# A mixture-of-experts kernel: the find products in fp32r over 128 rows, experts split over the halves of the partitions

## The chip, the cores and the metric

One Trainium2 chip, one of its cores. The metric is the kernel's time on the device in microseconds (us); the median of three runs before the change is 3870.12 us.

## The reference, cut to what matters

One layer on x of shape (4, 2048, 512), so 8192 tokens: a state-space part (layer norm, convolution, projections, a scan over the sequence), and then a mixture of experts with a shared expert. The second part is what the change touches:

```python
idx_flat = topk_idx.reshape(-1)                  # 8 of 64 experts per token
sort = jnp.argsort(idx_flat)
tok = sort // TOPK
x_sorted = x_flat[tok]
group_sizes = jnp.bincount(idx_flat, length=e).astype(jnp.int32)
g = jax.lax.ragged_dot(x_sorted, we_gate, group_sizes)
u = jax.lax.ragged_dot(x_sorted, we_up, group_sizes)
o = jax.lax.ragged_dot(jax.nn.silu(g) * u, we_down, group_sizes)
w_sorted = topk_w.reshape(-1)[sort].astype(o.dtype)
y = jnp.zeros_like(x_flat).at[tok].add(o * w_sorted[:, None])
```

All of it is float32.

## The kernel before, in words

The work goes in stages, one after the other, each a block of its own in which all engines run. `constants` makes index rows and masks. `ssm_inputs` and `scan_states` do the state-space part. `token_tiles` goes through 16 groups of four tiles of 128 tokens: it finishes the layer's first half, does the shared expert, picks the experts, and counts. `tile_table` turns the counts into a table of up to 576 expert tiles. `expert_tiles` goes through these 576 tiles, each 128 places of one expert.

**Counting.** The 8192 tokens are 64 blocks of 128. For every group of `token_tiles`, `count` multiplies the 0/1 matrix of chosen experts by a triangle: for each block, expert and slot, how many tokens of the block up to that slot chose the expert, less the same of the block before. ScalarE copies the sums out of PSUM (`keep_counts`, L939), SyncE stores them in DRAM as `rank_counts` (`store_counts`, L672). At the end `load_ranks` (L676) reads them back with the block as the partition: `k.ranks`, [64 blocks, 64 experts, 130], bfloat16; two more columns per expert hold a count of what lies ahead and a step in token numbers. The loads come in two parts: blocks 0 to 55 before the last two groups' counts are stored, the last eight after. Behind them in SyncE's order are the stores of the last two groups' weights (L668); the last of these waits for GpSimd's `weigh` (L747).

**The table.** `tile_table` begins with three products of `k.ranks`' last count column (L1291 to L1293), on which VectorE's first step (L1213) waits. Later two pairs of products (L1300, L1302) spread each expert's begin over its tiles; VectorE makes `k.begin` [64, 640] (L1284) and `k.rank` [128, 640] (L1286) of them.

**Finding.** For each expert tile the kernel must find which 128 tokens it holds. `mark` (L1727, VectorE, four tiles at once) compares each slot's number with `k.begin` and writes `past`, [64 blocks, 4 tiles, 128 slots] of 0 and 1 in bfloat16. `find` (L1535, TensorE) multiplies it for each tile by `k.ranks` of the tile's expert, 64 rows, 128 columns of weights, 130 moving columns, into `ps_find`. The expert's number is read by TensorE's sequencer out of the table (`expert_of`). `pick` (L1734 to L1743, VectorE) turns the sums into token numbers, for two tiles at once.

**The expert tile.** TensorE's order is written out by hand in `step`: `turn_x` of the next tile (four fp32 transposes, L1523), then in every fourth step `find` for four tiles twelve ahead, `gate_up` of this tile (twelve fp32r products of 512 columns, L1553, in three quarters: high by high, high by low, low by high), `turn_h` of the tile before (two transposes, L1582), `down` of the one before that (six products, L1572). Products in full accuracy are sums of three fp32r ones, with weights and inputs split into a high and a low part by ScalarE (L1632, L1640, L1656) and VectorE (L1695, L1703, L1709). SyncE loads new weights (L1460), GpSimd gathers the tokens' rows (L1489) and adds the results into the output (L1497). VectorE's order in `step` is: the low part of the next x, the low parts of new weights, then at s == 1 and s == 3 `pick`, at s == 2 `mark`, then `hidden` (L1715), `keep_h_low`, `scale` (L1722). Three groups of `mark`, `find` and `pick` stand ahead of the loop as a prologue.

```python
pe.wait_ge(marked, i + SHORT)
after(pe, picked, i)
for t, e in enumerate(experts):
    last = nc.tensor.matmul(ps_find[t // 2][:, t % 2, :], past[:, t, :],
                            k.ranks[:, bass.ds(e, 1), :].rearrange("j o t -> j (o t)"), ...)
```

Of the kernel before, what the change touches and what calls it, by code (L numbers as in the profile page):

```python
# [34 lines left out]
NEG = -3.0e38  # L35

# [19 lines left out]
def constants(nc, k):  # L56

    with ExitStack() as ctx:
        ahead_i = ctx.enter_context(nc.sbuf_tensor("ahead_i", [NB, NB], I32))
        ahead = ctx.enter_context(nc.sbuf_tensor("ahead", [NB, NB], F32))  # L60
        left_i = ctx.enter_context(nc.sbuf_tensor("left_i", [NB, P], I32))
        row_i = ctx.enter_context(nc.sbuf_tensor("row_i", [P, TABLE], I32))
        rank_i = ctx.enter_context(nc.sbuf_tensor("rank_i", [P, TABLE], I32))
        slot_i = ctx.enter_context(nc.sbuf_tensor("slot_i", [NB, P], I32))
        block_i = ctx.enter_context(nc.sbuf_tensor("block_i", [NB, 1], I32))
        block_f = ctx.enter_context(nc.sbuf_tensor("block_f", [NB, 1], F32))
        in_group = ctx.enter_context(nc.sbuf_tensor("in_group", [NB, 1], F32))
        is_first = ctx.enter_context(nc.sbuf_tensor("is_first", [NB, 1], F32))
        step = ctx.enter_context(nc.sbuf_tensor("step", [NB, 1], F32))
# [31 lines left out]
        def _(dve):  # L101
# [4 lines left out]
            nc.vector.tensor_scalar(ahead[:], ahead_i[:], 0.0, None, ALU.max)  # L106
            nc.vector.tensor_copy(k.left[:], left_i[:])
# [19 lines left out]
            nc.vector.tensor_copy(k.ranks[:, :, P + 1], step[:].to_broadcast([NB, E]))  # L127
# [406 lines left out]
def token_tiles(nc, k):  # L534
# [3 lines left out]
    with ExitStack() as ctx:  # L538
# [54 lines left out]
        counts = sb("counts", [E, 2, SUB, P], BF16)  # L593
# [62 lines left out]
        def _(sp):  # L656
# [18 lines left out]
            def load_ranks(at, to):  # L675
                sp.dma_start(k.ranks[at:to, :, 0:P], k.counts[at:to]).then_inc(ranks_loaded, 16)  # L676
# [43 lines left out]
            sp.wait_ge(ranks_loaded, 32)  # L720
# [430 lines left out]
def tile_table(nc, k):  # L1151
# [4 lines left out]
    with ExitStack() as ctx:  # L1156
# [32 lines left out]
        base = sb("base", [E, NB])  # L1189
# [5 lines left out]
        ps_step = ps("ps_step", [NB, E])  # L1195
        ps_turned = ps("ps_turned", [E, 2, P])
        ps_begin = [ps(f"ps_begin{i}", [NB, 512]) for i in range(2)]
# [3 lines left out]
        totalled = ctx.enter_context(nc.semaphore("q_totalled"))  # L1201
        upto_made = ctx.enter_context(nc.semaphore("q_upto_made"))
# [7 lines left out]
        def _(v):  # L1210
# [31 lines left out]
            nc.vector.tensor_scalar(base[:], ps_base[:], begins[:], None, ALU.add).then_inc(begins_made, 1)  # L1242
# [39 lines left out]
            for i, (at, to) in enumerate(((0, 512), (512, TABLE))):  # L1282
                v.wait_ge(spread_out, 2 * i + 2)
                nc.vector.scalar_tensor_tensor(out=k.begin[:, at:to], in0=k.tile_row[0:NB, at:to], scalar=float(-P),  # L1284
# [4 lines left out]
        def _(pe):  # L1289
            totals = k.ranks[:, :, P - 1]  # L1290
            nc.tensor.matmul(ps_total[:], k.left[:], totals, start=True, stop=True).then_inc(totalled, 1)  # L1291
            nc.tensor.matmul(ps_base[:], totals, k.ahead[:], start=True, stop=True).then_inc(totalled, 1)
            nc.tensor.matmul(ps_step[:], k.is_ahead[:], totals, start=True, stop=True).then_inc(totalled, 1)  # L1293
# [5 lines left out]
            for i, (at, to) in enumerate(((0, 512), (512, TABLE))):  # L1299
                nc.tensor.matmul(ps_begin[i][:, 0:to - at], base[:], of_tile[:, at:to], start=True,  # L1300
                                 stop=True).then_inc(spread_out, 1)
                nc.tensor.matmul(ps_first[i][:, 0:to - at], begins_row[:], of_tile[:, at:to], start=True,  # L1302
                                 stop=True).then_inc(spread_out, 1)
# [10 lines left out]
def expert_tiles(nc, k):  # L1314
# [8 lines left out]
    with ExitStack() as ctx:  # L1323
# [25 lines left out]
        past = sb("past", [NB, SHORT, P], BF16)  # L1349
# [165 lines left out]
        def _(pe):  # L1515
# [10 lines left out]
            def expert_of(i):  # L1526
                return pe.snap(entry(pe, i, 0, 2 * WSLOTS * E - 1) // (2 * WSLOTS), min_val=0, max_val=E - 1)
# [161 lines left out]
        def _(v):  # L1689
# [35 lines left out]
            def mark(i):  # L1725

                nc.vector.tensor_tensor(past[:], k.slot_row[:].unsqueeze(1).to_broadcast([NB, SHORT, P]),  # L1727
                                        k.begin[:, bass.ds(i, SHORT)].unsqueeze(2).to_broadcast([NB, SHORT, P]),
# [150 lines left out]
```

## Time and profile before

| | us |
|---|---|
| median of three runs | 3870.12 |
| lowest, highest | 3867.17, 3877.96 |
| the profiled execution | 3868.12 |
| its span in the trace | 3866.4 |
| mean granted TensorE clock | 0.973 |

How to read it: PE is TensorE's matmuls, PEld its weight loads, which overlap the matmuls; DVE is VectorE, ACT ScalarE, POOL GpSimd, SP SyncE; a q behind a name is that engine's sequencer. Matmuls are pipelined: their starts are recorded, their ends are modelled, so the length of one says less than the distance from start to start. In a merged row "x4" four follow each other, and the length is from the first one's start to the last one's modelled end. True fp32 products show as two records of weight load and two of matmul each, fp32r and bfloat16 products and transposes as one.

### The profile page before, as it was taken

How to read it: one execution, taken by the hardware profiler on the slowest of the kernel's cores; microseconds unless marked ns; L12 is line 12 of the kernel's file. 1: busy time of each engine (PE TensorE's matmuls, PEld its weight loads, DVE VectorE, ACT ScalarE, POOL GpSimd, SP SyncE). 2: the span in 40 equal slices, each digit the busy share in tenths (PEclk: the TensorE clock that was granted, in tenths of full speed). 3: DMA queues.
4: the chain of work that ended last, by engine and by line, in shares of the span. 5: the costliest groups of instructions: out<-in, count | busy, mean ns of one | idle time of the engine just before them, and what ended most of it. 6: DMA issues, size and time to landing. Idle time of an engine off the chain costs nothing.

```text
span 3866.4 us, 111487 instructions
## 1 busy us (share of the span) xinstructions
PE 3562.0 (92%) x17240; PEld 2854.9 (74%) x17241; DVE 2334.4 (60%) x5857; ACT 1389.3 (36%) x4103; POOL 1688.9 (44%) x1372
## 2 busy tenths in 40 slices
PE   5929888679999999999999899999999999999996
PEld 3417777558777877887888687888887877787785
DVE  5467777555666665666555655666555566566553
ACT  2234333223334333343333433333333333334331
POOL 1011111135555554555555454555555555555543
PEclk9969999889999999999999999999999999999998
DMA  3323333246667666676666666666666677667654
GB/s 125 102 82 120 113 110 106 77 104 135 135 146 174 142 137 139 123 172 151 123 124 154 159 116 129 142 139 139 126 142 121 142 159 164 136 126 169 122 102 74
DMA packets 216893, 502.58 MB, mean 130 GB/s; under 512 B 46847, under 2 KB 46975, under 8 KB 216456
## 3 DMA queue, kind: packets, MB, share of 16 engines
q0 software_dynamic: 129024, 320.94, 43.8%
q1 hardware_dynamic: 86472, 176.21, 13.6%
q10 hardware_dynamic: 1344, 4.85, 0.4%
q8 instruction: 18, 0.29, 0.0%
q14 instruction: 35, 0.29, 0.0%
HBM read 1115.79 MB, written 191.41 MB: 338 GB/s over the span
## 4 chain that ended last, share of the span: by engine, by line
PE 61%; DVE 5%; issue 5%; ACT 3%; DVEq 2%; DMA 2%; ACTq 2%; POOLq 0%; POOL 0%; SPq 0%
PE e_ps_gu L1553 35%; PE e_ps_y L1572 16%; PE e_ps_x L1523 5%; DVE e_w_low L1695 3%; PE e_ps_h L1582 3%; ACT e_w_high L1632 2%; PE e_ps_find L1535 2%; DMA out<-e_y,e_y_ids 1%; DVEq L1417 1%; ACTq L1417 1%; DVE e_past L1727 1%; DVE e_y L1722 1%; DVE e_below L1738 0%; DVEq L1695 0%; ACT e_xT_high L1640 0%
## 5 line engine op out<-in xcount | busy, mean ns | idle before, releaser
L1497 POOL DMA_INDIRECT out<-e_y,e_y_ids x576 | 956.3, 1660 | 1319.4 <-ACT e_weight L1644 603.7
L1553 PE MATMUL e_ps_gu<-e_w_high,e_xT_high 128*128 x2304 | 688.7, 419 | 15.6 <-issue 6.0
L1489 POOL DMA_INDIRECT e_x<-token_rows,e_x_ids x576 | 610.4, 1060 | 205.9 <-issue 172.8
L1553 PE MATMUL e_ps_gu<-e_w_low,e_xT_high 128*128 x2304 | 648.4, 400 | 6.3 <-issue 4.7
L1553 PE MATMUL e_ps_gu<-e_w_high,e_xT_low 128*128 x2304 | 653.0, 402 | 0.9 <-issue 0.6
L1722 DVE TENSOR_SCALAR e_y<-e_ps_y,e_weight 128x512 f32 (+1 forms) x576 | 431.0, 748 | 254.1 <-PE e_ps_y L1572 249.4
L1703 DVE TENSOR_TENSOR e_xT_low<-e_ps_x,e_xT_high 128x512 fp32r<-128x512 f32 x576 | 397.6, 690 | 266.5 <-ACT e_xT_high L1640 185.9
L1553 PEld LDWEIGHTS e_ps_gu<-e_w_high,e_xT_low 128*128 128x128 f32 x2304 | 430.8, 190 | 129.5 <-issue 29.2
L1553 PEld LDWEIGHTS e_ps_gu<-e_w_low,e_xT_high 128*128 128x128 f32 x2304 | 429.9, 189 | 126.7 <-issue 31.3
L1651 ACT ACTIVATE e_silu<-e_ps_gu 128x256 f32<-128x256 f32 x576 | 221.2, 384 | 827.3 <-PE e_ps_gu L1553 790.8
L1553 PEld LDWEIGHTS e_ps_gu<-e_w_high,e_xT_high 128*128 128x128 f32 x2304 | 396.5, 191 | 98.4 <-issue 37.4
L1640 ACT CAST e_xT_high<-e_ps_x 128x512 fp32r<-128x512 f32 x576 | 336.5, 584 | 302.1 <-PE e_ps_x L1523 301.4
L1572 PE MATMUL e_ps_y<-e_w_high,e_hT_high 128*128 x1152 | 411.6, 438 | 0.0
L1715 DVE TENSOR_TENSOR e_h<-e_silu,e_ps_gu 128x256 f32<-128x256 f32 x576 | 241.7, 420 | 280.6 <-ACT e_silu L1651 268.7
L1523 PEld LDWEIGHTS e_ps_x<-ident,e_x 128*128 128x128 f32 x2304 | 366.7, 204 | 54.9 <-issue 5.2
L1523 PE MATMUL e_ps_x<-ident,e_x 128*128 128x128 f32 x2304 | 366.0, 281 | 5.2 <-DVE e_xT_low L1703 5.0
L1572 PE MATMUL e_ps_y<-e_w_high,e_hT_low 128*128 x1152 | 362.8, 396 | 0.0
L1572 PE MATMUL e_ps_y<-e_w_low,e_hT_high 128*128 x1152 | 362.4, 396 | 0.0
L1660 ACT CAST e_x_ids<-e_tile_ids (+1 forms) x576 | 110.1, 192 | 506.1 <-issue 393.7
L1582 PEld LDWEIGHTS e_ps_h<-ident,e_h 128*128 128x128 f32 x1152 | 226.5, 197 | 53.0 <-DVE e_h L1715 4.5
L1695 DVE TENSOR_TENSOR e_w_low<-e_w_raw,e_w_high x128 | 226.0, 1766 | 50.9 <-issue 26.6
L1572 PEld LDWEIGHTS e_ps_y<-e_w_high,e_hT_low 128*128 128x128 f32 x1152 | 218.1, 189 | 51.1
(284 smaller groups left out, 4123.1 us busy)
## 6 DMA issues: line engine op xcount, KB each, us to landing
e_w_raw<-in_L_ffn_we_gate SPq DMA_DIRECT2D x576, 512.0 KB
e_w_raw<-in_L_ffn_we_up SPq DMA_DIRECT2D x576, 512.0 KB
e_w_raw<-in_L_ffn_we_down SPq DMA_DIRECT2D x576, 512.0 KB
a_x<-in_L_attn_x SPq DMA_DIRECT2D x64, 256.0 KB, 3.4
t_x_in<-in_L_attn_x SPq DMA_DIRECT2D x64, 256.0 KB, 2.7
token_rows<-t_xn SPq DMA_DIRECT2D x64, 256.0 KB, 2.0
out<-t_y_out SPq DMA_DIRECT2D x64, 256.0 KB, 2.1
e_x<-token_rows,e_x_ids POOLq DMA_INDIRECT x576
```

The lines of the kernel that those rows point to most:

```text
L1489: pool.indirect_dma_start(x[:, s % XS, :], None, k.rows, bass.IndirectOffsetOnAxis(x_ids[:, s:s + 1], 0)) \
L1497: pool.indirect_dma_start(k.out, bass.IndirectOffsetOnAxis(y_ids[:, s:s + 1], 0), y[:, s % YS, :], None, compute_op=ALU.add).then_inc(adde ...
L1523: last = nc.tensor.transpose(ps_x[:, c, :], chunks[:, c, :], k.ident[:])
L1553: last = nc.tensor.matmul(ps_gu[s % 2][:], x[:, s % 2, c, :], w[:, c], start=(n == 0), stop=(n == 3 * DC - 1))
L1572: last = nc.tensor.matmul(ps_y[s % 2][:], x[:, s % 2, c, :], w[:, c], start=(n == 0), stop=(n == 3 * FC - 1))
L1582: last = nc.tensor.transpose(ps_h[:, c, :], chunks[:, c, :], k.ident[:])
L1640: nc.scalar.copy(xT_high[:, s % 2], ps_x[:]).then_inc(xT_high_ready, 1)
L1651: nc.scalar.activation(silu[:, s % 2, :], ps_gu[s % 2][:, 0, :], ACT.Silu).then_inc(silu_ready, 1)
L1695: split_weights(v, words, s, lambda half, place: nc.vector.tensor_tensor(w_low[:, bass.ds(place, 1), PARTS[part]], w_raw[:, bass.ds(half, ...
L1703: nc.vector.tensor_tensor(xT_low[:, s % 2], ps_x[:], xT_high[:, s % 2].bitcast(F32), ALU.subtract).then_inc(xT_low_ready, 1)
L1715: nc.vector.tensor_tensor(h[:, s % 2, :], silu[:, s % 2, :], ps_gu[s % 2][:, 1, :], ALU.mult).then_inc(h_made, 1)
L1722: nc.vector.tensor_scalar(y[:, bass.ds(slot, 1), :].rearrange("p o d -> p (o d)"), ps_y[s % 2][:], weight[:, s % SHORT:s % SHORT + 1], Non ...
```

## The change

The counts stay in float32 from PSUM to SBUF, and `k.ranks` becomes fp32r. Its 128 partitions are now the 64 blocks twice: the lower 64 hold experts 0 to 31, the upper 64 experts 32 to 63, [128, 32, 130], so it takes as many bytes per partition as before. `past` becomes [128, 4, 128] in fp32r, and a find product goes over 128 rows; of the half of the rows that belong to the other experts, `k.begin` is 2^20 too large, so that `past` is 0 there (`not_half`, added to `base`). `expert_of` takes the expert's number modulo 32. The first products of the table become fp32 ones, two of 64 rows each, and the constants for them are made for 128 partitions. Each load of the ranks becomes two, one for each half.

```diff
--- before.py
+++ after.py
@@ constants
...
-        left_i = ctx.enter_context(nc.sbuf_tensor("left_i", [NB, P], I32))
+        left_i = ctx.enter_context(nc.sbuf_tensor("left_i", [P, P], I32))
...
-            nc.vector.tensor_scalar(ahead[:], ahead_i[:], 0.0, None, ALU.max)
-            nc.vector.tensor_copy(k.left[:], left_i[:])
+            for rows, first in ((slice(0, NB), 0.0), (slice(NB, P), float(NB))):
+                nc.vector.tensor_scalar(ahead[rows], ahead_i[rows], first, 0.0, ALU.add, ALU.max)
+            nc.vector.tensor_scalar(block_i[:], block_i[:], NB - 1, None, ALU.bitwise_and)
+            for half in range(2):
+                for other in range(2):
+                    nc.vector.memset(k.not_half[E // 2 * half:E // 2 * half + E // 2, other, :], FAR * (half != other))
+            dve.drain()
+            for rows, first in ((slice(0, NB), 0.0), (slice(NB, P), float(NB))):
+                nc.vector.tensor_scalar(k.left[rows], left_i[rows], first, None, ALU.add)
...
@@ token_tiles
-        counts = sb("counts", [E, 2, SUB, P], BF16)
+        counts = sb("counts", [E, 2, SUB, P])
...
-                sp.dma_start(k.ranks[at:to, :, 0:P], k.counts[at:to]).then_inc(ranks_loaded, 16)
+                for half in range(2):
+                    sp.dma_start(k.ranks[NB * half + at:NB * half + to, :, 0:P].bitcast(F32),
+                                 k.counts[at:to, E // 2 * half:E // 2 * half + E // 2]).then_inc(ranks_loaded, 16)

...
-            sp.wait_ge(ranks_loaded, 32)
+            sp.wait_ge(ranks_loaded, 64)
...
@@ tile_table
-        base = sb("base", [E, NB])
+        base = sb("base", [E, 2, NB])
-        ps_step = ps("ps_step", [NB, E])
+        ps_step = ps("ps_step", [P, E // 2])
-        ps_begin = [ps(f"ps_begin{i}", [NB, 512]) for i in range(2)]
+        ps_begin = [ps(f"ps_begin{i}", [P, 512]) for i in range(2)]
+        half_totalled = ctx.enter_context(nc.semaphore("q_half_totalled"))

...
-            nc.vector.tensor_scalar(base[:], ps_base[:], begins[:], None, ALU.add).then_inc(begins_made, 1)
+            nc.vector.scalar_tensor_tensor(out=base[:], in0=ps_base[:].unsqueeze(1).to_broadcast([E, 2, NB]),
+                                           scalar=begins[:], in1=k.not_half[:], op0=ALU.add,
+                                           op1=ALU.add).then_inc(begins_made, 1)

...
-                nc.vector.scalar_tensor_tensor(out=k.begin[:, at:to], in0=k.tile_row[0:NB, at:to], scalar=float(-P),
+                nc.vector.scalar_tensor_tensor(out=k.begin[:, at:to], in0=k.tile_row[:, at:to], scalar=float(-P),
-            totals = k.ranks[:, :, P - 1]
-            nc.tensor.matmul(ps_total[:], k.left[:], totals, start=True, stop=True).then_inc(totalled, 1)
-            nc.tensor.matmul(ps_base[:], totals, k.ahead[:], start=True, stop=True).then_inc(totalled, 1)
-            nc.tensor.matmul(ps_step[:], k.is_ahead[:], totals, start=True, stop=True).then_inc(totalled, 1)
+            totals = k.ranks[:, :, P - 1].bitcast(F32)
+            halves = [(slice(NB * half, NB * half + NB), slice(E // 2 * half, E // 2 * half + E // 2)) for half in range(2)]
+            for half, (blocks, experts) in enumerate(halves):
+                after(pe, half_totalled, half)
+                nc.tensor.matmul(ps_total[:, experts], k.left[blocks], totals[blocks], start=True,
+                                 stop=True).then_inc((half_totalled, totalled)[half], 1)
+            for blocks, experts in halves:
+                last = nc.tensor.matmul(ps_base[experts], totals[blocks], k.ahead[blocks], start=True, stop=True)
+            last.then_inc(totalled, 1)
+            for blocks, experts in halves:
+                last = nc.tensor.matmul(ps_step[blocks], k.is_ahead[blocks], totals[blocks], start=True, stop=True)
+            last.then_inc(totalled, 1)
-                nc.tensor.matmul(ps_begin[i][:, 0:to - at], base[:], of_tile[:, at:to], start=True,
+                nc.tensor.matmul(ps_begin[i][:, 0:to - at], base[:].rearrange("e h j -> e (h j)"), of_tile[:, at:to], start=True,

...
@@ expert_tiles
-        past = sb("past", [NB, SHORT, P], BF16)
+        past = sb("past", [P, SHORT, P], F32R)

...
-                return pe.snap(entry(pe, i, 0, 2 * WSLOTS * E - 1) // (2 * WSLOTS), min_val=0, max_val=E - 1)
+                return pe.snap(entry(pe, i, 0, 2 * WSLOTS * E - 1) // (2 * WSLOTS) & (E // 2 - 1), min_val=0, max_val=E // 2 - 1)

...
-                nc.vector.tensor_tensor(past[:], k.slot_row[:].unsqueeze(1).to_broadcast([NB, SHORT, P]),
-                                        k.begin[:, bass.ds(i, SHORT)].unsqueeze(2).to_broadcast([NB, SHORT, P]),
+                nc.vector.tensor_tensor(past[:], k.slot_row[:].unsqueeze(1).to_broadcast([P, SHORT, P]),
+                                        k.begin[:, bass.ds(i, SHORT)].unsqueeze(2).to_broadcast([P, SHORT, P]),

...
@@ program
-        k.counts = nc.dram_tensor("rank_counts", [NB, E, P], BF16).ap()
+        k.counts = nc.dram_tensor("rank_counts", [NB, E, P], F32).ap()
-        k.slot_row = sb("slot_row", [NB, P])
+        k.slot_row = sb("slot_row", [P, P])
-        k.ranks = sb("ranks", [NB, E, P + 2], BF16)
-        k.begin = sb("begin", [NB, TABLE])
+        k.ranks = sb("ranks", [P, E // 2, P + 2], F32R)
+        k.begin = sb("begin", [P, TABLE])

...
-            k.ahead = sb("ahead_bf", [NB, NB], BF16)
-            k.is_ahead = sb("is_ahead", [NB, NB], BF16)
-            k.left = sb("left", [NB, P], BF16)
+            k.ahead = sb("ahead", [P, NB])
+            k.is_ahead = sb("is_ahead", [P, NB])
+            k.left = sb("left", [P, P])
+            k.not_half = sb("not_half", [E, 2, NB])

...
```

## Rows read from the trace of the kernel before

**Rows 1.** The page, part 1, TensorE's row: busy us, share of the span, instructions.
```profile
PE 3562.0 (92%) x17240; PEld 2854.9 (74%) x17241; DVE 2334.4 (60%) x5857; ACT 1389.3 (36%) x4103; POOL 1688.9 (44%) x1372
```
**Rows 2.** The page, part 4, the chain that ended last: by engine, by line.
```profile
PE 61%; DVE 5%; issue 5%; ACT 3%; DVEq 2%; DMA 2%; ACTq 2%; POOLq 0%; POOL 0%; SPq 0%
PE e_ps_gu L1553 35%; PE e_ps_y L1572 16%; PE e_ps_x L1523 5%; DVE e_w_low L1695 3%; PE e_ps_h L1582 3%; ACT e_w_high L1632 2%; PE e_ps_find L1535 2%; DMA out<-e_y,e_y_ids 1%; DVEq L1417 1%; ACTq L1417 1%; DVE e_past L1727 1%; DVE e_y L1722 1%; DVE e_below L1738 0%; DVEq L1695 0%; ACT e_xT_high L1640 0%
```
**Rows 3.** Timeline of PE, 857 to 873 us: start us, length us, engine, line, instruction.
```profile
859.62 0.63 PE L1523 MATMUL e_ps_x<-ident,e_x 128*128 128x128 f32 x4
860.18 0.40 PE L1535 MATMUL e_ps_find<-ranks,e_past 64*128 x4
860.51 1.20 PE L1553 MATMUL e_ps_gu<-e_w_high,e_xT_high 128*128 x4
861.55 1.10 PE L1553 MATMUL e_ps_gu<-e_w_low,e_xT_high 128*128 x4
...
865.06 0.63 PE L1523 MATMUL e_ps_x<-ident,e_x 128*128 128x128 f32 x4
865.45 1.17 PE L1553 MATMUL e_ps_gu<-e_w_high,e_xT_high 128*128 x4
866.46 1.10 PE L1553 MATMUL e_ps_gu<-e_w_low,e_xT_high 128*128 x4
```
**Rows 4.** Line 1535 (find): count, length min/median/max in ns, first and last start.
```profile
L1535 PEldq FUSED_REGOPS  x580: 81/84/119, 790.7 to 3782.3; - x194
...
L1535 PE MATMUL e_ps_find<-ranks,e_past x580: 214/217/284, 790.9 to 3783.9; 64*128 x194
```
**Rows 5.** Waits of PE, 800 to 3820 us: us in total, times, longest.
```profile
PE e_ps_find L1535 <- DVE e_past L1727: 26.8, 34, 2.7
```
**Rows 6.** Groups by line and form: count, busy us, mean ns, idle before, releaser.
```profile
L1523 PE MATMUL e_ps_x<-ident,e_x 128*128 128x128 f32 x2304 | 366.0, 281 | 5.2 <-DVE e_xT_low L1703 5.0
...
L812 PE MATMUL t_ps_r<-w_r,t_xT 128*128 128x64 f32 x512 | 66.4, 273 | 14.2 <-ACT t_xT L914 14.2
...
L1572 PEld LDWEIGHTS e_ps_y<-e_w_high,e_hT_high 128*128 128x128 f32 x1152 | 180.0, 196 | 0.2
```
**Rows 7.** Timeline of PE, 500 to 512 us, the router's product in true fp32.
```profile
504.85 1.00 PE L812 MATMUL t_ps_r<-w_r,t_xT 128*128 128x64 f32 x8
```
**Rows 8.** Timeline of PEld, 1995.6 to 1996.4 us, first weight loads of `down`.
```profile
1995.76 0.31 PEld L1572 LDWEIGHTS e_ps_y<-e_w_high,e_hT_high 128*128 128x128 f32 x2
```
**Rows 9.** The tile e_past: count, length min/median/max in ns.
```profile
L1727 DVE TENSOR_TENSOR e_past<-slot_row,begin x145: 677/684/752, 787.9 to 3781.0; 64x512 bf16<-64x512 f32 x145
```
**Rows 10.** The page, part 5, a 128x512 fp32r result on VectorE.
```profile
L1703 DVE TENSOR_TENSOR e_xT_low<-e_ps_x,e_xT_high 128x512 fp32r<-128x512 f32 x576 | 397.6, 690 | 266.5 <-ACT e_xT_high L1640 185.9
```
**Rows 11.** Waits over the whole span, VectorE's first in `ssm_inputs`.
```profile
DVE a_win L241 <- DMA a_b_pair<-in_L_attn_b_in: 9.2, 1, 9.2
```
**Rows 12.** Timeline, 735 to 800 us: end of the token stage, start of the table.
```profile
748.50 1.01 SPq L676 DMA_DIRECT2D ranks<-rank_counts  x1
...
758.58 0.76 SPq L676 DMA_DIRECT2D ranks<-rank_counts  x1
...
764.64 0.61 POOL L747 TENSOR_TENSOR t_weights<-t_picked,t_total 128x256 f32<-128x256 f32 x1 [12.90 <-DMA token_rows<-t_weights]
...
768.75 0.27 PE L1291 MATMUL q_ps_total<-ranks,left 64*128 64x64 bf16 x1 [20.46 <-PEq L538]
...
770.67 0.42 PE L1295 MATMUL q_ps_turned<-ident,q_upto 128*64 128x128 f32 x1 [1.29 <-DVEq L1221]
```
**Rows 13.** DMA, 749.6 to 757.9 us: ranks and last counts, packets of 256 B.
```profile
DMA packets 4153, 1.05 MB, mean 127 GB/s; under 512 B 4151, under 2 KB 4151, under 8 KB 4153
```
**Rows 14.** Windows: start:end, length, busy of five engines, PEclk, DMA share, GB/s.
```profile
748.40:749.50 1.10, 0.00 (x0) 0.00 (x0) 0.00 (x0) 0.51 (x1) 0.77 (x3) 0.50 0.56 212
```
**Rows 15.** Timeline of PE, 146 to 160 us: 512-column products in true fp32.
```profile
145.42 10.03 PE L300 MATMUL a_product<-a_xnT,a_wtap 128*128 128x512 f32 x23
155.29 1.91 PE L290 MATMUL a_turned<-ident,a_xn 128*128 128x128 f32 x16
```

More of the change, by code:

```diff
@@ L35 @@
 NEG = -3.0e38
+FAR = float(1 << 20)
 class Shared:
@@ L58, in constants @@
     with ExitStack() as ctx:
-        ahead_i = ctx.enter_context(nc.sbuf_tensor("ahead_i", [NB, NB], I32))
-        ahead = ctx.enter_context(nc.sbuf_tensor("ahead", [NB, NB], F32))
-        left_i = ctx.enter_context(nc.sbuf_tensor("left_i", [NB, P], I32))
+        ahead_i = ctx.enter_context(nc.sbuf_tensor("ahead_i", [P, NB], I32))
+        ahead = ctx.enter_context(nc.sbuf_tensor("ahead_f", [P, NB], F32))
+        left_i = ctx.enter_context(nc.sbuf_tensor("left_i", [P, P], I32))
         row_i = ctx.enter_context(nc.sbuf_tensor("row_i", [P, TABLE], I32))
         rank_i = ctx.enter_context(nc.sbuf_tensor("rank_i", [P, TABLE], I32))
[L64 to L69, printed above, removed]
+        slot_i = ctx.enter_context(nc.sbuf_tensor("slot_i", [P, P], I32))
+        block_i = ctx.enter_context(nc.sbuf_tensor("block_i", [P, 1], I32))
+        block_f = ctx.enter_context(nc.sbuf_tensor("block_f", [P, 1], F32))
+        in_group = ctx.enter_context(nc.sbuf_tensor("in_group", [P, 1], F32))
+        is_first = ctx.enter_context(nc.sbuf_tensor("is_first", [P, 1], F32))
+        step = ctx.enter_context(nc.sbuf_tensor("step", [P, 1], F32))
         made = ctx.enter_context(nc.semaphore("consts_made"))
@@ L126, in _ @@
             dve.drain()
-            nc.vector.tensor_copy(k.ranks[:, :, P + 1], step[:].to_broadcast([NB, E]))
+            nc.vector.tensor_copy(k.ranks[:, :, P + 1], step[:].to_broadcast([P, E // 2]))
         @block.sync
```

## The prediction, made before the change was run

> **What bounds the kernel now.** I read the page first: TensorE is busy 92% of the span [rows 1]. The chain that ended last runs through its matmuls for 61% of the span; PE's sequencer is nowhere in the chain's list, and e_ps_find L1535, the product that the change rewrites, stands in it with 2% [rows 2]. So in the expert stage (from about 800 us to the end) PE sets the pace, and what leaves PE's stream counts, unless PE is waiting there anyway.
>
> Then PE's timeline over a step with finding and one without [rows 3]. Without: transposes start at 865.06, gate/up at 865.45, its second quarter at 866.46, together 1.40 us. With: transposes at 859.62, four find products at 860.18, gate/up at 860.51, its second quarter at 861.55, together 1.93 us. Finding costs 0.53 us of the path. There are 580 find products, so 145 groups [rows 4]; three stand in the prologue, 142 in the stream. They are worth 75 us, the most that any edit of find could give. The products themselves take 4 x 0.06 us of the 0.53: four are 0.40 long, one is 0.217 [rows 3, 4], (0.40 - 0.217) / 3 = 0.06. The other 0.29 us lie at entry and exit: find starts 0.56 after the transposes did, where gate/up starts 0.39 after them; and behind find gate/up starts 0.33 after four products of 0.06 began, and its first quarter takes 1.04 instead of 1.01.
>
> The waits of PE show where it isn't the pace: in 34 groups find waited for DVE's e_past, 26.8 us in all [rows 5].
>
> **A find group after the change.** Removed: four bf16 products over 64 rows, with the gaps around them. Added: four fp32r products over 128 rows, 130 columns each. I take the gaps as the cost of going from 128-row products to 64-row ones and back: both neighbours are 128*128 and find alone is 64*128 [rows 3]. The Trainium skill (TensorEngine Tiling (Array Packing), section Key Properties) says that a change of tiling mode drains the engine. The gap agrees, though nothing here has yet parted rows from type.
>
> The price of the new product is unknown: no fp32r product under 512 columns is in the trace. From rows: fp32 weights of 128x128 follow each other at 0.104 us (t_ps_r: eight take 1.00, one 0.273, 0.727 / 7) [rows 6, 7], at 0.116 (transposes: four take 0.63, one 0.281) [rows 3, 6] and, as fp32r, at 0.114 (two loads take 0.31, one 0.196) [rows 6, 8]. The moving side is no bound if it is one pass: 512 columns come at 1.01 / 4 = 0.25 us [rows 3], so 130 need 0.064. A new product then costs what its weight load costs, 0.104 to 0.12; I take 0.112, near the fp32r row. Four are 0.448 in place of 0.53: 0.082 saved. In the 108 groups that don't wait that is **8.9 us**. In the 34 that wait, the entry gap already lies under the wait and no load is pulled ahead: 0. Bounds: 0.104 in all 142 groups saves 16.2; 0.12 in 108 saves 5.4.
>
> One rule of the Trainium skill speaks against the change (TensorE: Matmul & The Clock Gate, sections LDWEIGHTS and Weight-path perf modes): a load takes its columns over 1.2 GHz, and 2-byte weights of 128 columns load faster, where fp32 gains nothing. By its figure, an estimate, a product would be 0.107 us, the group 0.43 and the saving 11.0 us.
>
> **The edits beside it.** DVE's mark writes 128x512 fp32r for 64x512 bf16: 0.684 now [rows 9], and e_xT_low, of just the new output shape, is 0.690 [rows 10]; nothing, at worst 34 x 0.006 = 0.2. The expert's number takes one more register operation on PE's sequencer, whose L1535 operations take 0.084 [rows 4]; the cover is that the sequencer runs ahead (no PEq in [rows 2]). With the cover gone, four a group would cost 0.34, 48 us over 142. The added constants (seven small DVE operations and drains) are covered by DVE's 9.2 us wait for the first weights [rows 11]; without it they would be some 1.5 us. ACT's copy of the counts writes 4 bytes for 2 of the same 64x512, and the counts' stores double inside a stage whose queue is mostly free: nothing there.
>
> **The end of the token stage** is where the change costs. SP loads the ranks (748.50), stores the last two groups' counts behind them in the same queue, gets to the last ranks at 758.58, then stores the weights; POOL's t_weights at 764.64 waits for such a store, and PE's first product of the table (768.75) for all [rows 12]. Each delay there delays everything. The 256 B packets become 512 B, their number stays. Now 4153 packets, 1.05 MB, go at 127 GB/s [rows 13]: 2.0 ns each. The output's rows of 2 KB go at 212 GB/s [rows 14]: 9.7 ns each. On the line between these, 512 B take 3.1 ns, 1.1 more: +4.5 us for the 4153 and +0.6 for the last load's 512. Bounds: the same rate of packets, 0; the same rate of bytes, +8.3 and +1.0. Each rank load becomes two issues; the extra one before the weights' stores costs the 0.76 of its row [rows 12], the other is under the transfers (0 to 1.0). The table's three bf16 products become six fp32 ones, and the second of the first pair waits for the first's end (half_totalled). Behind that wait on PE stand the other four, which VectorE needs only for base, some 5 us later; on the path is the pair alone: 0.27 now, twice an fp32 one, whose nearest row is 0.42 and which has a second record [rows 12]: +0.7 (0.3 to 1.2). Sum **+6.6 us**, bounds +1.1 and +12.3.
>
> The Trainium skill (DMA: Bandwidth & Descriptors, section Specifications) says that transfers reach line rate from 512 B, and that below it there is a read-modify-write. By that rule a 512 B packet would take no longer than a 256 B one, and the sum would come out 5.1 us lower. The two rates above can't tell.
>
> **Sum.** -8.9 + 6.6 = -2.3 us on the profiled execution's own 3868.12: 3865.8. It lies 2.0 below the median of the three runs, 3870.12, so on the median **3867.8**. This case's own range: -16.2 + 1.1 = -15.1, 3855; -5.4 + 12.3 = +6.9, 3877. A measurement of this kernel can tell about 0.3% (11.6 us) from no change, so the case is mostly "no change": the gaps go, slower loads take back most of them, and the stage before takes the rest.
>
> **The rivals.**
> *Short fp32r products are no single pass (slower).* If the product of 130 columns ran like true fp32 it would be two records. One of 512 columns takes (155.29 - 145.42) / 23 = 0.429 us [rows 15], so 130 columns take 0.109, as long as a load; a product 0.22, a group 0.88: +0.35 in 108 groups, +0.45 in the 34, 53 us, and with the stage's 6.6 **3930**. For it: nothing shows fp32r below 512 columns. Against: there it has one record of 0.25 where fp32 has two of 0.429, and nothing hints at a dependence on width. The group turns from gain to loss at 0.1325 us a product (0.53 / 4), the kernel already at 0.117 (6.6 / 432 less).
> *The gaps stay*, so the change doesn't do what it says. A group then costs 0.29 + 0.45 = 0.74, +0.21 x 142 = +30, with the stage **3907**. For it: the gaps are never seen without find, whose operands lie in other memory than its neighbours'. Against: from fp32 transposes to fp32r gate/up there is no gap (0.39 is less than four times 0.116).
> *Loads hide (faster).* If fp32r weights came as fast as the bf16 ones, the group were 0.24: -0.29 x 142 = -41, **3836** with the stage. Against: no fp32 load under 0.104 anywhere.
> *The mark gets later*: 0.1 us more on each of the 34 waits would be 3.4 us, 3871.
>
> **Chances.** Forecast 0.72 (0.14 of it below -11.6, 0.56 within, 0.02 above), short products doubled 0.10, gaps stay 0.08, loads hide 0.07, mark later 0.03 (0.01 within, 0.02 above). Faster 0.21, same 0.57, slower 0.22. The forecast's 3855 to 3877 holds about 0.7, so the range reaches up to the gaps' case, 3907, and to 3853 below.
>
> **What would show it.** In PE's timeline: find x4 as 128*128, transposes to second quarter of gate/up in 1.40 + 0.45 = 1.85 us. Eight find records a group would prove the first rival, 2.14 us the second, 1.64 the third. In the waits: e_past in 34 groups, as now. At the stage's end: the last rank load at about 763 for 758.58, the table's first product at 775 for 768.75; 770 would mean that the packets' number counts. The prediction is wrong if all before 800 us moves by over 12 us, or a find group by over 0.13.

## The result, and the profile of the changed kernel

| | before | after |
|---|---|---|
| median of 4 runs, us | 3872.47 | 3902.19 |
| lowest, highest | 3867.17, 3877.96 | 3901.4, 3904.36 |
| span of the profiled execution | 3866.4 | 3899.7 |
| mean granted TensorE clock | 0.973 | 0.968 |

The ratio is 1.0078 [1.006, 1.0095]: the change makes the kernel some 30 us slower.

The first column holds one run more than the table ahead of the prediction. The page of after, TensorE's row of part 1 and the chain's engines of part 4 (as in [rows 1, 2]):

```profile
PE 3589.4 (92%) x17249; PEld 2900.5 (74%) x17250; DVE 2336.9 (60%) x5864; ACT 1390.4 (36%) x4103; POOL 1681.0 (43%) x1372
...
PE 61%; issue 5%; DVE 5%; DMA 3%; DVEq 2%; ACT 2%; ACTq 1%; POOLq 0%; POOL 0%; SPq 0%
```

They look as before. Nine matmuls and nine loads more, so short fp32r products aren't split in two. PE's sequencer is still missing from the chain; the cause below hides inside "PE". The steps seen on PE's timeline of after, a step with finding that doesn't wait, for [rows 3] (start, length, engine, line, instruction):

```profile
862.91 0.63 PE L1544 MATMUL e_ps_x<-ident,e_x 128*128 128x128 f32 x4
863.30 1.17 PE L1574 MATMUL e_ps_gu<-e_w_high,e_xT_high 128*128 x4
864.31 1.10 PE L1574 MATMUL e_ps_gu<-e_w_low,e_xT_high 128*128 x4
...
867.83 0.63 PE L1544 MATMUL e_ps_x<-ident,e_x 128*128 128x128 f32 x4
868.22 0.65 PE L1556 MATMUL e_ps_find<-ranks,e_past 128*128 x4
868.69 1.14 PE L1574 MATMUL e_ps_gu<-e_w_high,e_xT_high 128*128 x4
869.67 1.10 PE L1574 MATMUL e_ps_gu<-e_w_low,e_xT_high 128*128 x4
```

Transposes to second quarter take 1.84 us with finding (869.67 - 867.83), 1.40 without: 0.44 a group for 0.53 before, and find starts 0.39 behind the transposes where it started 0.56 behind. This part of the prediction came out. A group that did have to wait for `mark` looks otherwise. First one of before, then one of after, each on PE's timeline (the bracket is the wait and its releaser):

```profile
1005.49 0.71 PE L1535 MATMUL e_ps_find<-ranks,e_past 64*128 x4 [0.85 <-DVE e_past L1727]
1006.32 1.19 PE L1553 MATMUL e_ps_gu<-e_w_high,e_xT_high 128*128 x4
```

```profile
1014.36 1.30 PE L1556 MATMUL e_ps_find<-ranks,e_past 128*128 x4 [1.14 <-DVE e_past L1748]
1015.70 1.19 PE L1574 MATMUL e_ps_gu<-e_w_high,e_xT_high 128*128 x4
```

Before, gate/up starts 0.83 us after the first find product; now 1.34. The product itself is no such length: take the last one's modelled length off the merged row, and the starts before lie (0.71 - 0.225) / 3 = 0.16 apart, after (1.30 - 0.323) / 3 = 0.33, three times what they take when nothing waited: there four products and the entry to gate/up take 0.47, 0.12 each. What stands between them is on PE's sequencer. Line 1535 before, 1004 to 1007 us (engine, operation, count, length min/median/max in ns, first and last start; PEldq is TensorE's sequencer as it stands in the rows of the weight loads):

```profile
L1535 PEldq FUSED_REGOPS  x4: 81/87/96, 1005.3 to 1005.8; - x4
...
L1535 PE MATMUL e_ps_find<-ranks,e_past x4: 224/225/225, 1005.5 to 1006.0; 64*128 x4
```

The same of after, line 1556, 1014 to 1016 us:

```profile
L1556 PEldq ALU_OP  x8: 36/41/46, 1014.1 to 1015.1; - x8
L1556 PEldq FUSED_REGOPS  x4: 46/46/46, 1014.3 to 1015.2; - x4
...
L1556 PE MATMUL e_ps_find<-ranks,e_past x4: 322/323/325, 1014.4 to 1015.3; 128*128 x4
```

Four register instructions became twelve. The division that gives the expert's number, the index into `k.ranks` and the address were one fused instruction a product; with `& (E // 2 - 1)` between division and multiplications they are two single ones and a fused one. Twelve lie between 1014.1 and 1015.2: 0.1 us from start to start, although each lasts 0.04. The first instruction of the group is the one that waits for `mark`: in all 34 such groups of either trace it starts 0.04 us behind the end of `mark`, and the group's other register instructions start behind it. In the waits of PE, the row of [rows 5] is now

```profile
PE e_ps_find L1556 <- DVE e_past L1748: 37.5, 36, 2.9
```

By my count of the starts, the first product comes over 0.3 us behind the last transpose in 34 groups of the stream, in both kernels; these are "the 34" from here on.

**Where the 33 us between the two profiled executions are.** From the starts of all matmuls of the two traces: the expert loop (first transpose to last `down` product) takes 3057.2 us for 3032.4, +24.8; what stands ahead of it, counted from the first rank load, +7.5, of which +1.7 in the prologue's find groups. Over the 142 groups of the stream I summed the stretch from the last transpose to the second gate/up product:

| us over all groups | before | after |
|---|---|---|
| 108 groups that don't wait | 95.0 | 87.7 |
| 34 that wait: last transpose to first find product | 36.5 | 41.8 |
| ... first find product to first gate/up product | 28.6 | 45.6 |
| ... first to second gate/up product | 11.4 | 12.7 |
| sum | 171.5 | 187.8 |

The saving in the 108 is there, -7.3. The 34 lose 23.6, of which 17.0 in their products (0.84 a group becomes 1.34). The row above it grows by 5.3, and that isn't a later `mark`: from the waiting register instruction to the first product it takes 5.3 us over the 34 before and 10.5 after, one instruction or three ahead of the product, while the end of `mark` lies only 0.3 us later, summed over the 34. So 22.2 of the 23.6 us are the register instructions. By whole cycles of four steps: those with a waiting group go from 22.33 to 23.19 us (+0.86, 34 times +29), the others from 20.61 to 20.57 (-4). So the 34 lose 6 us more outside the stretch. They are in the gate/up that follows: its twelve products take 2.9 to 3.1 us (first start to the next product behind them) or 4.2 to 5.3, nothing between, and behind the 34 groups the long sort is there 3 times before and 11 times after. On average it takes 3.09 before and 3.44 after, +12 over the 34. The cycles lose only 6 outside the stretch, so later steps give back about half. What makes the long ones long is shown with the second experiment.

The end of the token stage on after's timeline, for [rows 12]:

```profile
749.76 1.77 SPq L685 DMA_DIRECT2D ranks<-rank_counts  x2
...
764.05 0.69 SPq L685 DMA_DIRECT2D ranks<-rank_counts  x2
...
771.13 0.61 POOL L757 TENSOR_TENSOR t_weights<-t_picked,t_total 128x256 f32<-128x256 f32 x1 [18.13 <-DMA token_rows<-t_weights]
...
775.24 1.30 PE L1307 MATMUL q_ps_total<-ranks,left 64*128 64x32 f32 x4 [25.68 <-PEq L546]
...
777.89 0.42 PE L1316 MATMUL q_ps_turned<-ident,q_upto 128*64 128x128 f32 x1 [0.63 <-DVEq L1232]
```

and its DMA, 751.2 to 764 us, for [rows 13]:

```profile
DMA packets 4170, 2.10 MB, mean 164 GB/s; under 512 B 74, under 2 KB 4170, under 8 KB 4170
```

The first load is 1.3 us later in this execution than in the one of before, and not by the change (it stands ahead of everything that the change lengthens), so I count from it. The last load comes 14.29 us behind the first for 10.08, +4.2; the first product of the table another 11.19 behind for 10.17, +1.0; `q_ps_turned` 2.65 for 1.92, +0.7; the rest of the table -0.2; the prologue's find groups +1.7.

### The profile page after: what moved, and what is told of

Same layout as the page of the kernel before. It is cut to its first block, busy times and chain, and to the rows that moved or that the text cites. A ratio compares the mean times of both kernels' runs of the same rounds, so it can differ in the third digit from the quotient of the medians.

```text
span 3899.7 us, 112675 instructions
## 1 busy us (share of the span) xinstructions
PE 3589.4 (92%) x17249; PEld 2900.5 (74%) x17250; DVE 2336.9 (60%) x5864; ACT 1390.4 (36%) x4103; POOL 1681.0 (43%) x1372
## 4 chain that ended last, share of the span: by engine, by line
PE 61%; issue 5%; DVE 5%; DMA 3%; DVEq 2%; ACT 2%; ACTq 1%; POOLq 0%; POOL 0%; SPq 0%
PE e_ps_gu L1574 34%; PE e_ps_y L1593 16%; PE e_ps_x L1544 5%; DVE e_w_low L1716 3%; DMA out<-e_y,e_y_ids 3%; PE e_ps_h L1603 3%; PE e_ps_find L1556 2%; ACT e_w_high L1653 1%; DVEq L1438 1%; DVE e_past L1748 1%; DVE e_y L1743 1%; ACTq L1438 0%; DVE e_below L1759 0%; DVEq L1716 0%; DMA e_w_raw<-in_L_ffn_we_down 0%
## 5 line engine op out<-in xcount | busy, mean ns | idle before, releaser
L1518 POOL DMA_INDIRECT out<-e_y,e_y_ids x576 | 945.7, 1642 | 1350.6 <-ACT e_weight L1665 647.1
```

What stands on the lines that cost most here:

```text
L1518: pool.indirect_dma_start(k.out, bass.IndirectOffsetOnAxis(y_ids[:, s:s + 1], 0), y[:, s % YS, :], None, compute_op=ALU.add).then_inc(adde ...
```

## The experiments

**The theory** after this reading: where PE is fed ahead, register instructions cost nothing; where find stands at `mark`'s wait, its sequencer stands too, and each product then comes at their pace. Rivals: the fp32r load costs 0.33 us by itself when nothing hides it; and `mark` comes later.

**1. The changed kernel, the expert's number from the table.** A fourth field of the tile table holds the expert modulo 32; TensorE reads it as it is.

```diff
-                return pe.snap(entry(pe, i, 0, 2 * WSLOTS * E - 1) // (2 * WSLOTS) & (E // 2 - 1), ...)
+                return pe.snap(entry(pe, i, 3, E // 2 - 1), ...)
...
+            nc.vector.tensor_scalar(upper[:], expert[:], float(E // 2), float(-(E // 2)), ALU.is_ge, ALU.mult)
+            nc.vector.tensor_tensor(table[:, :, 3], expert[:], upper[:], ALU.add)
```

> The changed kernel, but the expert's number modulo 32 comes ready out of a fourth field of the tile table, so that each find product has one fused register operation ahead of it, as before the change, instead of three. Theory S (sequencer): in the 34 groups in which find waits for the mark, PE's queue is empty and a product costs the time of its register operations, 0.16 us with one and 0.33 with three. Then these products come at 0.16 to 0.17 us, which takes 34 x 4 x 0.165 = 22 us off, and up to 6 more behind them: 3872 to 3882 for 3902. Rival L (load): an fp32r product whose weights were not pulled ahead costs 0.33 by itself. Then the 0.33 stay and the time is 3898 to 3903. Rival D (later mark): the loss is in the length of the waits; 3895 to 3903.

Measured: 3867.11 us (3864.76 to 3872.39), 0.9987 [0.9978, 0.9997] of before: 35 us less than after, 5 us below the range expected, and just below before. Line 1559 over the whole span, and a waiting group on PE's timeline:

```profile
L1559 PEldq FUSED_REGOPS  x580: 46/46/56, 798.0 to 3778.1; - x194
...
991.28 0.70 PE L1559 MATMUL e_ps_find<-ranks,e_past 128*128 x4 [0.33 <-DVE e_past L1751]
991.99 1.19 PE L1577 MATMUL e_ps_gu<-e_w_high,e_xT_high 128*128 x4
```

Gate/up 0.71 behind the first product for 1.34. The 34 groups' products fall from 45.6 to 24.0 us, and of their gate/ups none is long. The stretch ahead of the first product falls too, from 41.8 to 32.9. The load is fp32r as before, and the rival that it costs 0.33 by itself falls. So does the rival of the later `mark`: it still writes 128 rows of fp32r here.

**2. The kernel before with a mask that changes nothing.** All the rest of before stays, bf16 and 64 rows.

```diff
-                return pe.snap(entry(pe, i, 0, 2 * WSLOTS * E - 1) // (2 * WSLOTS), min_val=0, max_val=E - 1)
+                return pe.snap(entry(pe, i, 0, 2 * WSLOTS * E - 1) // (2 * WSLOTS) & (E - 1), min_val=0, max_val=E - 1)
```

> The kernel before, with '& 63' behind the expert's number: nothing computed changes, but three register operations stand ahead of each find product. Theory S: bf16 products over 64 rows come at 0.33 us in the waiting groups instead of 0.16, 0.06 elsewhere as now; +20 to +30 us, 3891 to 3901 for 3871. Rival L and rival D: no change, 3868 to 3875.

Measured: 3919.53 (3918.07 to 3926.91), 1.0125 [1.0108, 1.0142]. One `&` makes the old kernel 46 us slower, more than the whole change did and more than expected. Line 1535 over the whole span, and a waiting group on the timeline:

```profile
L1535 PEldq ALU_OP  x1160: 36/41/56, 794.2 to 3834.9; - x194
L1535 PEldq FUSED_REGOPS  x580: 46/46/56, 794.4 to 3835.0; - x194
...
1011.60 1.21 PE L1535 MATMUL e_ps_find<-ranks,e_past 64*128 x4 [1.15 <-DVE e_past L1727]
1012.93 1.20 PE L1553 MATMUL e_ps_gu<-e_w_high,e_xT_high 128*128 x4
```

(1.21 - 0.22) / 3 = 0.33 us a product, in bf16 over 64 rows as in fp32r over 128, and 1.33 to gate/up. The 34 groups' products take 45.7 us, as in after. The stretch ahead of the first product grows from 36.5 to 43.0, with the `mark` of before. Of the 46 us the find stretches hold 26.7 (171.5 to 198.2), which is about what was expected; the loop grew by 47.8. The other 20 go with TensorE's clock. The windows of this kernel around the group above (start:end, length, busy us of PE, PEld, DVE, ACT, POOL, granted clock, DMA share, GB/s):

```profile
1010.00:1011.60 1.60, 0.45 (x5) 0.26 (x4) 1.03 (x3) 0.68 (x2) 0.68 (x1) 1.00 0.92 175
1011.60:1012.90 1.30, 0.90 (x4) 0.36 (x4) 1.30 (x3) 0.06 (x1) 0.00 (x0) 1.00 1.05 405
1012.90:1014.00 1.10, 1.07 (x5) 0.90 (x6) 0.39 (x2) 0.13 (x1) 0.00 (x0) 1.00 0.99 378
1014.00:1015.40 1.40, 1.40 (x5) 1.13 (x4) 1.12 (x2) 0.00 (x0) 1.13 (x1) 0.57 1.01 401
1015.40:1017.50 2.10, 2.10 (x8) 1.54 (x6) 0.94 (x6) 0.09 (x1) 1.79 (x2) 0.50 0.59 155
```

PE waits for 1.15 us, then dribbles four find products over 1.3 us with its loads busy for only 0.36, and at about 1014 us the granted clock falls from 1.00 to 0.50, 2.4 to 1.2 GHz, and stays there through the last row: most of a gate/up at half the clock. In the group of after shown above, with the same 0.33 a product, it stayed at 1.00. All six kernels in which find waits show what goes with the fall (bf16_128_rows and bf16_128_rows_number are experiments 5 and 6; the wait is the stretch from the last transpose to the first find product):

| | products of the 34, us | mean gate/up behind them, us | long ones, wait under 1.5 us | long ones, wait over 1.8 us |
|---|---|---|---|---|
| before | 28.6 | 3.09 | 0 of 31 | 3 of 3 |
| number_from_table | 24.0 | 2.96 | 0 of 31 | 0 of 3 |
| bf16_128_rows_number | 24.2 | 3.07 | 0 of 31 | 3 of 3 |
| after | 45.6 | 3.44 | 9 of 31 | 2 of 3 |
| mask_in_before | 45.7 | 3.86 | 18 of 31 | 3 of 3 |
| bf16_128_rows | 45.7 | 3.46 | 9 of 31 | 3 of 3 |

In these 204 groups each of the 50 long gate/ups lies over a stretch at 0.50, by 2.6 us or more, and none of the other 154 touches one. Behind the usual waits, under 1.5 us, the clock fell only where the products came at the slow pace, in 36 of 93 groups, and in none of 93 at the fast one. Behind the three longest waits of a kernel it fell at either pace, though not once in number_from_table.

0.77 us by 34 is 26 us for the mask, 6 of which later steps give back (outside the find stretches its cycles with a waiting group are 0.58 us longer, 34 times 20). Each of the slow kernels differs from a fast one in the register instructions, so they bring the falls with them; whether it is the pace of the products or the 0.15 us more ahead of the first was not parted.

**3 and 4. `mark` one step earlier**, in the changed kernel and in the one before, so that find waits for nobody:

```diff
-                if s == 2 and exists(i - s + AHEAD_FIND):
+                if s == 1 and exists(i - s + AHEAD_FIND):
                     mark(i - s + AHEAD_FIND)
```

> The changed kernel, with VectorE's mark one step earlier (at s == 1, right behind the pick that frees the tile). All theories: the waits for e_past go in most of the 34 groups, and these groups cost what the others cost, 0.81 us from the last transpose to the second gate/up product instead of 2.94 on average. That is 34 x 2.13 = 72 us if all of them go and nothing else becomes late: 3830; where the wait only turns into another one (VectorE's hidden layer later, transposes of h later), 3860 to 3900. Theory S says besides that the spacing of 0.33 is gone from every find group that doesn't wait.

> The kernel before with the same earlier mark. 34 groups now cost 2.25 us from the last transpose to the second gate/up product, the others 0.88: up to 34 x 1.37 = 46 us off, 3825. Beside the changed kernel with the earlier mark it shows what the change is worth when nobody waits: a find group 0.08 shorter, 142 x 0.08 = 11.4 us, less the 8.8 us that everything ahead of the expert stage lost: 0 to 5 us in favour of the changed one.

Measured: changed 3839.21 (3836.53 to 3840.02), 0.9911 [0.9895, 0.9928], 63 us off of the 72 at most that were expected; before 3836.26 (3833.95 to 3837.7), 0.9904 [0.9887, 0.992]. In the waits of PE the row of e_past is gone from the old kernel and is almost gone from the changed one:

```profile
PE e_ps_find L1556 <- DVE e_past L1748: 5.3, 2, 2.8
```

With the wait, the gap of 30 us between the kernels goes down to 3, though the changed kernel still has its 580 x 3 register instructions: where PE is fed ahead they cost next to nothing (experiment 7 has a number for it). The 3 us lie within the noise, the two intervals overlap, so the medians can't tell +3 from the -2.3 of the prediction. The two traces can, part by part: the changed kernel's loop is 4.6 us shorter (2992.1 for 2996.7), and what stands ahead of it, from the first rank load, 7.3 longer (57.8 for 50.5). The old kernel alone gained 36 us and not the 46 expected. Its steps without find went from 5.080 to 5.116 us on average: part of what the waits free is given back elsewhere (see behind experiment 8).

**5. bf16 over 128 rows.** The change with its type undone and its rows kept; the `&` is still in it.

```diff
-        past = sb("past", [P, SHORT, P], F32R)
+        past = sb("past", [P, SHORT, P], BF16)
...
-        k.ranks = sb("ranks", [P, E // 2, P + 2], F32R)
+        k.ranks = sb("ranks", [P, E // 2, P + 2], BF16)
```

(the counts, their DRAM tensor and the three constants go back to bf16 in the same way.)

> The changed kernel with counts, ranks, past and the table's constants back in bfloat16, everything else as changed: 128 rows, experts split over the halves, number modulo 32 by '&'. It parts rows from type. If the 0.29 us at find's entry and exit came from the 64 rows, they stay away: a find group that doesn't wait costs 4 x 0.06 = 0.24 instead of 0.45, 108 x 0.21 = 23 us off, the ranks' packets are 256 B again (5 us off), the 34 waiting groups keep their 0.33 a product: 3870 to 3880. If they came from the change of type between bf16 and fp32r, they are back: a group 0.53, 3903 to 3910.

Measured: 3888.46 (3885.67 to 3890.97), 1.004 [1.0025, 1.0054]: 14 us below after, though above the 3870 to 3880 expected. PE's timeline, a group that doesn't wait:

```profile
859.90 0.63 PE L1544 MATMUL e_ps_x<-ident,e_x 128*128 128x128 f32 x4
860.37 0.39 PE L1556 MATMUL e_ps_find<-ranks,e_past 128*128 x4
860.57 1.18 PE L1574 MATMUL e_ps_gu<-e_w_high,e_xT_high 128*128 x4
861.59 1.10 PE L1574 MATMUL e_ps_gu<-e_w_low,e_xT_high 128*128 x4
```

Transposes to second quarter 1.69 us, 0.29 above a step without find, where before had 0.53 and after 0.44. Find still takes four bf16 products 0.06 apart ((0.39 - 0.22) / 3), and gate/up starts 0.20 behind it for 0.33. So the gaps came from the rows, not from the type; 128 rows remove most of them (the median whole step with a find that doesn't wait: 5.447 us before, 5.200 now, and 5.360 in after). Yet its 34 waiting groups take 45.7 us for their products, and 12 long gate/ups follow them: the pace of the three register instructions again, in a third combination of type and rows. With 256 B packets again and four rank loads still, the last load comes 9.6 us behind the first for 14.29 in after: the packets' size made the last load late, not the number of issues.

**6. The same with the number from the table** (5 and 1 together).

> The same with the number modulo 32 out of the table. Rows: 23 us for the find groups and 5 us for the packets off the fp32r kernel with the number from the table (3867), and the waiting groups at 0.12 to 0.16 a product: 3835 to 3843. Type: 3868 to 3875.

Measured: 3845.53 (3840.2 to 3850.51), 0.9926 [0.9909, 0.9942]. Against 5 the register instructions are worth 43 us here, against 1 the type is worth 22; 2.5 us above the range expected.

**7 and 8. All of it: the number from the table and the early mark**, on fp32r (after_number_early) and on bf16 over 128 rows (bf16_number_early).

> The changed kernel (fp32r, 128 rows) with the number out of the table and the earlier mark. Theory S: with the waits gone nobody stands behind the register operations in the loop, so the number brings little beside the earlier mark: 1.5 us in the prologue and some tenths elsewhere, 3833 to 3838 for the 3839 with the earlier mark alone. If it brings 20 us or more, the operations cost also where PE doesn't wait.

> All three: bfloat16 over 128 rows, number out of the table, mark one step earlier. Rows theory: 142 x 0.21 = 30 us and 5 us of packets below the fp32r kernel with both edits: 3798 to 3806, the fastest of all. Type theory: 3840 to 3846.

Measured: 3834.45 (3832.66 to 3836.09), 0.9902 [0.9885, 0.9918], as expected; the register instructions are worth 4.8 us where nothing waits for `mark`, 1.8 of them ahead of the loop. And **3817.49** (3815.17 to 3819.82), 0.9859 [0.9842, 0.9875], the best of all: 55 us faster than before, 85 faster than the change as made. It falls short of the 3798 to 3806 expected. Its find stretches did shrink to 91.6 us (171.5 before), a saving of 80, but the steps without find grew from 5.080 to 5.162. The waits of PE, 800 to 3800 us, of this kernel:

```profile
PE e_ps_gu L1577 <- issue: 20.1, 82, 0.6
PE e_ps_gu L1577 <- DVEq L1722: 10.5, 25, 1.2
```

On before_early_mark the first of these stands at 14.5 us in 66 waits, on after at 11.8 in 57. The faster PE gets through find, the more often gate/up stands waiting. In the 432 steps without find the twelve gate/up products take 24 us more in sum than before, of the 36 by which these steps grew. 31 of these gate/ups are over 4 us long (22 before), but not for the clock: only 1 of the 31 (2 of the 22) lies over a stretch at 0.50. The trace shows what stands in them. The sequencer reads an entry of the tile table between the third and fourth, sixth and seventh, or ninth and tenth product. One such place, PE's timeline and then the reading line, 1510.9 to 1511.9 us:

```profile
1510.69 0.96 PE L1577 MATMUL e_ps_gu<-e_w_high,e_xT_high 128*128 x3 [0.52 <-DVEq L1722]
1511.87 0.50 PE L1577 MATMUL e_ps_gu<-e_w_high,e_xT_high 128*128 x1 [0.22 <-issue]
```

```profile
L1441 PEldq FUSED_REGOPS  x2: 69/110/151, 1511.0 to 1511.5; - x2
L1441 PEldq TENSOR_LOAD <-tiles x1: 304/304/304, 1511.1 to 1511.1; - x1
L1441 PEldq SEQ_ASSERT  x1: 18/18/18, 1511.7 to 1511.7; - x1
```

Gate/up had just waited 0.52 us, three products came, and the fourth came 0.62 behind the third for the usual 0.25, right behind the last instruction of the reading. There are 163 such gaps over 0.1 us in this kernel at these three places, all of them with the end of a reading inside, 43.2 us in sum; before has 111 with 28.6 (109 with a reading), before_early_mark 130 with 33.6 (128). All 31 long gate/ups have one or more. It is the mechanism of find at another place: a sequencer that isn't ahead shows in PE's stream. That the readings cost this time was read from the traces and not tried.

| | `&` in find | number from table | table, early mark |
|---|---|---|---|
| fp32r, 128 rows | 3902.2 | 3867.1 | 3834.5 |
| bf16, 128 rows | 3888.5 | 3845.5 | 3817.5 |

The type alone costs 14 to 22 us in each column, the ranks' packets included. bf16 over 64 rows is 3872.5, 3919.5 with the `&`, and 3836.3 with the early mark. fp32r over 64 rows was not tried: `k.ranks` would take twice the bytes per partition, and there is no room in SBUF.

## Why the prediction was wrong

The forecast was 3867.8, no change. Measured is +30 us, slower. The time lies inside the range, but only because the range was stretched to the case "the gaps stay", which is not what happened.

- **The step that failed** is "In the 34 that wait, the entry gap already lies under the wait and no load is pulled ahead: 0", together with the pricing of the register operation beside it. The prediction gave its cover ("that the sequencer runs ahead") and its price without it ("four a group would cost 0.34"), and then took the cover as whole in all 142 groups because PEq is missing from the chain. But the waits, read just before, show 34 groups in which PE stands at find [rows 5]. There the sequencer stands too, for the wait is on the group's first register instruction, and it has nothing ahead. The price was too low as well: the `&` is not one operation of 0.084 more but breaks one fused instruction into three, spaced 0.1. Measured is +0.17 us a product (0.16 to 0.33), +0.5 a group, 17 us over the 34, and 5.2 more ahead of the first products; on their whole stretches +23.6 for the 0 forecast, and with the clock that falls behind some of them +29 over their cycles. The clock's price stood in no term at all. Run 2 shows the price without the rest of the change (+46), run 1 the change without the price (-35), runs 3 and 4 both kernels without the wait (3 us apart).
- **The other sign of it was in the row**: the four register operations of before lie 0.17 apart in a waiting group and the products 0.16. The 0.06 us of [rows 3] is the pace of a group that doesn't wait. A look at one of the 34 would have shown that the products there don't come at their own pace.
- **A find group that doesn't wait**: the forecast was 0.082 saved. Whole steps show 5.447 to 5.360, 0.087; the sum over the 108 is -7.3 for the -8.9. One record a product, 0.12 us apart on average (0.14 between the first two, 0.11 behind), near the weight loads of [rows 6, 8], as argued. One register instruction a product or three makes no difference to it (after and number_from_table).
- **The Trainium skill's rule on drains** (TensorEngine Tiling (Array Packing), section Key Properties), with which the gaps were read: run 5 parts rows from type and agrees. Going to 128 rows in bf16 makes a step with finding 0.25 us shorter (5.447 to 5.200).
- **The Trainium skill's rule on weight loads** (TensorE: Matmul & The Clock Gate, sections LDWEIGHTS and Weight-path perf modes), which spoke against the change: the trace comes near, products start 0.11 to 0.12 us apart for the estimate of 0.107, and bf16 ones 0.06. Of the 14 to 22 us between the two rows of the table above it can be a part only: the loops of the profiled executions differ by 6, 12 and 7 us from column to column, and what stands ahead of them, where the packets are, by 7, 7 and 9.
- **The token stage's end**: +6.6 forecast; measured +4.2, +1.0 and +0.7, less 0.2 in the rest of the table, and +1.7 in the prologue's three find groups, which I had left out: +7.5. The +1.7 is mostly the register instructions too: the old kernel with the mask has +1.5 there. A packet of 512 B took (12.8 us / 4170) 3.1 ns, the value on the line between [rows 13, 14].
- **The Trainium skill's 512 B rule** (DMA: Bandwidth & Descriptors, section Specifications), read as "no longer than a 256 B packet": the measurement decides against it. The rate of bytes rose from 127 to 164 GB/s, but the packet took 1.5 times as long, and going back to 256 B in run 5 took the time back.
- **The rivals.** "Short products are no single pass": false, one record each. "The gaps stay" named a time of 3907, near the measured one, by another mechanism: its sign was 2.14 us from transposes to second quarter, and 1.84 is measured. "Loads hide": false. "The mark gets later": the mark takes 693 ns for 684 and ends 0.3 us later in sum; the 5 us by which the waits grew are register instructions ahead of the first product (runs 1 and 2: less with one instruction, more with three, whatever `mark` writes).
- **Left open**: what decides, group by group, whether the clock falls at the slow pace; why the three longest waits of number_from_table left it at 1.00; and how much of the growth of the steps without find a kernel would get back whose sequencer read the table elsewhere. The readings account for 15 of the 36 us in the fastest kernel.

## What to carry to other kernels

"The sequencer runs ahead" must be checked where the engine waits, not over the span: at every wait in the stream the queue behind it can't be filled with what the sequencer still has to work out, each register instruction between short products then costs its 0.1 us, and the dribble can cost the clock besides. Reads of a table by the sequencer belong to the same count. So count them in the compiled program (a mask between a division and a multiplication can turn one into three), read addresses ready-made from a table, and move the wait away first; here the wait was worth more than what stood behind it. Where one edit carries a row count and a type, run each alone: the rows brought the gain and the type cost it.

## What of the hardware was not expected

- The register instructions of after's find last 36 to 56 ns each on PE's sequencer but start 0.1 us apart behind a wait. Their pace sets the pace of short products behind a wait, much the same whatever type and rows: 0.16 us with one of 0.087; 0.33 with three, in bf16 over 64 rows, bf16 over 128 and fp32r over 128; with one of 0.046, 0.14 in fp32r and 0.12 in bf16 over 128 rows.
- Behind a wait under 1.5 us and four find products at 0.33 the granted clock fell from 1.00 to 0.50 in 36 of 93 groups; at 0.12 to 0.18 a product in 0 of 93. A gate/up that it caught took 1.45 us longer (4.4 for 2.95).
- A read of one table entry on PE's sequencer (TENSOR_LOAD of 0.3 us with what follows it) made a gap in a stream of 0.25 us products in 109 places of before and 163 of the fastest kernel.
- Going from 128-row products to four of 64 rows and back costs some 0.25 us beside the products (runs before and 5, whole steps).
- fp32r with 130 moving columns is one record a product, 0.11 to 0.12 us apart, the pace of fp32 transposes and fp32r weight loads; bf16 in the same place 0.06.
- Packets of 512 B take 3.1 ns each on all queues together, of 256 B 2.0: neither the number of packets nor the bytes alone sets the time (windows of before and after at the token stage's end).
